# A fused four-layer kernel: attention diagonals as four products, low halves on GpSimd, row dispatch spread over the steps

## The chip, the cores and the metric

The kernel runs on one core of a Trainium2 chip. The metric is the device time of one execution in microseconds. Three runs of the kernel before gave 2604.55, 2605.08 and 2601.78 us. The names of the engines in the profile are PE (TensorE matmuls), PEld (its weight loads), DVE (VectorE), ACT (ScalarE), POOL (GpSimd) and SP (SyncE, which issues most transfers).

## The reference

4096 tokens (16 sequences of 256) of width 128 go through four layers. Every layer normalises its input and adds an attention block and a feed-forward block to it:

```python
xn = _layernorm(x)
x = x + attn_l(xn) + ffn_l(xn)
```

Layer 1 (index 0 in the reference and in the names `L0_...`) has no softmax over keys and a dense feed-forward. The other three have softmax attention with 16 heads in sequences of 256 and a mixture of 8 experts:

- layer 2 (`L1_...`): RMS norm, heads of 64, no mask, two experts of eight for each token;
- layer 3 (`L2_...`): heads of 8, causal mask, one expert for each token;
- layer 4 (`L3_...`): heads of 8 with rotary parts of 32 shared by the heads, causal mask, two experts and a shared one.

```python
probs = softmax(where(mask, (q @ k.T) * scale, -inf)); out = probs @ v
```

## The kernel before

Tokens are worked on in `NCH` = 8 chunks of 512 (two sequences). The stages of the layers with experts are named R, T, A, M and C with the layer index 1, 2 or 3 of the names in the code, so that the *second, third and fourth* layers are A1, A2 and A3: R and T route the tokens, A is the attention, M the experts, C the combination. `stage_closed` makes an engine wait until all engines have left a stage.

**The attention of a chunk** has `STEPS` = 16 steps, one for each pair of heads and sequence (two units a step). A step p goes through the engines like this:

- TensorE `maxima` computes the scores of step p once into the bank pair `duo`; VectorE `maxima` (line 1954) reduces them to the negated row maxima `nmax` (lines 1957 and 1958, in layer 2 line 2077), and makes from them the *diagonals*: the identity times each of four columns of maxima, f16, 128x512 (line 1961, in layer 2 line 2080). It is one `scalar_tensor_tensor` with two inputs in SBUF.
- TensorE `scores` (line 1292) waits for the diagonals, adds them by a matmul to the scores that are computed a second time, with keys on the partitions, in the banks `mo0`, `mo1` and `pt`. So the maximum is subtracted before the exponential.
- ScalarE `exps` (lines 903 and 904) writes each exponential twice, as f32 and as f16: the *high half*.
- The *low half* is the f32 value minus the high half, in f16, so that the products with the values are more exact than f16 alone. In layers 3 and 4 VectorE makes it for both units at once, 128x768 (`pair_low`, line 1967, instruction at 1969). In layer 2 GpSimd makes it, 128x512 for each unit (`prob_low`, line 635, instruction at 637).
- TensorE `average` (line 1318) multiplies both halves with the values into `ob` or `pt`, in small matmuls, once the low half is there. VectorE `scale_o` divides by the row sums.

The order is written out by hand on each engine. In step p of layers 3 and 4 TensorE does scores(p), maxima(p + 2), average(p - 1), then selections, projections or shared-expert work. VectorE does maxima(p + 2) and its diagonals, pair_low(p), then whatever belongs to the chunk (`scale_o`, the residual sum, `prepare` for the next chunk in steps 9 to 13, with the rotary parts of layer 4 at lines 1910 to 1928). ScalarE does exps(p), which waits for the low half of p - 2, since it reuses that buffer. The four halves of two steps share two buffers (`p % 2`).

In layer 2, where VectorE is at maxima(p + 1) in step p, GpSimd waits for the diagonals of step p + 1 before it starts the low halves of step p:

```python
if p + 1 < STEPS or more:
    at_step(diag_made, pool, stage, i, p + 1)
prob_low(i, p, 0)
prob_low(i, p, 1)
```

**Dispatch of rows.** After routing, every token's normalised row must go to the slots of its experts in `slot_rows` in HBM. `send_row_tile` (line 622) sends one tile of 128 rows with an indirect transfer issued by GpSimd. There are 64 tiles in layers 2 and 4 (two experts for each token) and 32 in layer 3. In layer 2 GpSimd sends four after the low halves of each step of the first chunk (`per_step` = 4). In layers 3 and 4 it does nothing else in the attention stage and sends all tiles as soon as the stage opens. SyncE waits for all of a layer's tiles (`rows_sent`) before it loads the next layer's expert weights over the buffer the tiles came from, and the experts stage waits for them too. After layer 3's dispatch GpSimd prepares rotary copies of weights (lines 682 to 684) that TensorE waits for at the start of layer 4's attention, and then sends the experts' results (`send_results`, line 662).

Of the kernel before, what the change touches and what calls it, by code (L numbers as in the profile page):

```python
# [22 lines left out]
ALU = mybir.AluOpType  # L23
# [7 lines left out]
P = 128  # L31
# [4 lines left out]
ALL = TOKENS // P  # L36
# [8 lines left out]
STEPS = 16  # L45
# [97 lines left out]
def build_program(nc, A, out):  # L143
    ctx = ExitStack()
    with ctx:
# [284 lines left out]
        def at_step(event, eng, stage, i, k):  # L430

            per = event.per[stage]
            if k < 0:
                i, k = i - 1, k + per
            elif k >= per:
                i, k = i + 1, k - per
            if not (isinstance(i, int) and i < 0):
                event.wait(eng, stage, i, k)

        def step1(event, eng, i, k):  # L440

            at_step(event, eng, "A1", i, k)
# [150 lines left out]
        def _(pool):  # L593
# [33 lines left out]
            def attention(layer):  # L627

                stage = f"A{layer}"
                stage_closed(pool, f"T{layer}")  # L630
                if layer == 1:
                    pool.wait_ge(blank_sent, 16 * 4 * len(TOP))
                per_step = TOP[layer] * ALL // STEPS

                def prob_low(i, p, h):
                    p_high.wait(pool, "A1", i, 2 * p + h)
                    pool.tensor_tensor(p16[:, p % 2, h, 1, :], p32[:, h, :], p16[:, p % 2, h, 0, :], ALU.subtract)\  # L637
                        .then_inc(p_low.sem, 1)

                def chunk(i, parity, more):  # L640
                    for p in range(STEPS):
                        if p + 1 < STEPS or more:
                            at_step(diag_made, pool, stage, i, p + 1)
                        prob_low(i, p, 0)
                        prob_low(i, p, 1)
                        if isinstance(i, int) and i == 0:
                            for n in range(per_step * p, per_step * p + per_step):
                                send_row_tile(layer, n // ALL, n % ALL)

                if layer == 1:  # L650
                    chunks1(pool, chunk)
                else:
                    for n in range(per_step * STEPS):
                        send_row_tile(layer, n // ALL, n % ALL)

            def send_results(layer):
                def step(s, half, b, first):
# [937 lines left out]
        def _(dve):  # L1595
# [290 lines left out]
            def attention(layer):  # L1886
# [67 lines left out]
                def maxima(i, p):  # L1954

                    max_full.wait(dve, stage, i, 2 * p + 1)
                    dve.tensor_reduce(nmax4[:, p % 2, 0:2], duo[:, :, 0:P], AX.X, ALU.max, negate=True)  # L1957
                    dve.tensor_reduce(nmax4[:, p % 2, 2:4], duo[:, :, P:LINE], AX.X, ALU.max, negate=True)\  # L1958
                        .then_inc(nmax_made.sem, 1)
                    nmax_made.wait(dve, stage, i, p)  # L1960
                    dve.scalar_tensor_tensor(  # L1961
                        out=diag2[:, p % 2, :, :, :].rearrange("p q h c -> p (q h) c"),
                        in0=ident[:, :].rearrange("p (o c) -> p o c", o=1).broadcast_to([P, 4, P]), scalar=1.0 / 16,
                        in1=nmax4[:, p % 2, :].rearrange("p (a o) -> p a o", o=1).broadcast_to([P, 4, P]),
                        op0=ALU.mult, op1=ALU.mult).then_inc(diag_made.sem, 1)

                def pair_low(i, p):
                    p_high.wait(dve, stage, i, 2 * p + 1)
                    dve.tensor_tensor(p16_2[:, p % 2, 1, :], p32_2[:, p % 2, :], p16_2[:, p % 2, 0, :], ALU.subtract)\  # L1969
                        .then_inc(p_low.sem, 1)  # L1970

                def scale_o(i, g):

# [18 lines left out]
                def chunk(i, parity, more):  # L1992
                    begun = not (isinstance(i, int) and i == 0)
                    for p in range(STEPS):
                        if p + 2 < STEPS:
                            maxima(i, p + 2)
                        elif more:
                            maxima(i + 1, p + 2 - STEPS)
                        pair_low(i, p)
                        if p and p % 4 == 0:  # L2000
                            scale_o(i, p // 4 - 1)
                        elif p == 0 and begun:
                            scale_o(i - 1, 3)
                        if p == 2 and begun:
                            add(acc_full, x_made, i - 1, 0)
                        if p == 8 and layer == 3:
                            if begun:
                                x_made.wait(dve, stage, i - 1)
                            add(sh_down, sh_added, i, FB - 1)
                        if more:  # L2010
                            prepare(i + 1, 1 - parity, p)
                    if not more:
                        scale_o(i, 3)
                        if layer == 3:
                            sh_added.wait(dve, stage, i)
                        add(acc_full, x_made, i, 0)
# [202 lines left out]
```

## Time and profile before

| | before |
|---|---|
| median of 3 runs | 2604.55 us |
| lowest and highest | 2601.78 and 2605.08 us |
| the profiled execution's own time | 2598.39 us |
| its span in the profile | 2596.6 us |
| mean granted TensorE clock | 0.883 |
| TensorE matmuls busy | 2019.9 us (78%) |
| TensorE weight loads busy | 1394.1 us (54%) |
| VectorE busy | 1908.6 us (74%) |
| ScalarE busy | 1377.8 us (53%) |
| GpSimd busy | 723.5 us (28%) |

The table is of one execution, taken by the hardware profiler. Weight loads overlap matmuls. Matmul ends are modelled, and spans on GpSimd are rough. The span is the time from the first to the last instruction of the program; the execution's own time is 1.8 us longer. TensorE's clock is given as a share of its full speed. In the rows below, a line of the timeline gives start, duration, engine, source line, operation, output <- inputs, shape and count of merged instructions, and in brackets how long the engine was idle before and who released it. DVEq, SPq and so on are an engine's sequencer.

### The profile page before, as it was taken

What the parts mean: (1) busy time and instruction counts of PE and PEld (TensorE: products, weight loads), DVE (VectorE), ACT (ScalarE), POOL (GpSimd) and SP (SyncE); (2) the same over time, 40 slices, a digit from 0 to 9 for tenths busy, and PEclk for the clock granted to TensorE, in tenths of its full rate; (3) what the DMA queues carried; (4) which work ended last, traced back from release to release, by engine and by line L of the source; (5) the groups of instructions that cost most, each with busy time, mean ns of one, the idle gap of its engine ahead of it and who ended that gap; (6) DMA issues with size and microseconds to landing.
All of it is one profiled execution on the core that took longest, in us unless ns stands there. A gap on an engine that the chain in (4) does not pass through costs nothing.

```text
span 2596.6 us, 65873 instructions
## 1 busy us (share of the span) xinstructions
PE 2019.9 (78%) x23246; PEld 1394.1 (54%) x23247; DVE 1908.6 (74%) x4031; ACT 1377.8 (53%) x2794; POOL 723.5 (28%) x674
## 2 busy tenths in 40 slices
PE   1543679999999788815888887863899999998993
PEld 0213346666666566714555554543566666665662
DVE  2236667878788788866999998766677777776775
ACT  0231346767677655502766666430566666665552
POOL 0012685545455333323300000340720000000552
PEclk9775889999999999965988987885899998998997
DMA  8900012000000011220200000120100000000224
GB/s 226 168 0 0 26 37 72 2 3 3 3 2 2 10 48 49 61 73 15 85 2 2 2 2 5 48 64 12 51 18 2 2 2 2 2 2 10 63 62 124
DMA packets 109664, 88.07 MB, mean 34 GB/s; under 512 B 11240, under 2 KB 95816, under 8 KB 109424
## 3 DMA queue, kind: packets, MB, share of 16 engines
q1 hardware_dynamic: 97840, 60.82, 9.8%
q0 software_dynamic: 11584, 23.91, 2.7%
q8 instruction: 168, 2.75, 0.4%
q14 instruction: 72, 0.59, 0.1%
HBM read 45.26 MB, written 39.43 MB: 33 GB/s over the span
## 4 chain that ended last, share of the span: by engine, by line
PE 48%; DVE 28%; issue 12%; POOL 6%; ACT 3%; DMA 2%; DVEq 1%; SPq 1%; ACTq 0%; POOLq 0%
PE duo L1020 11%; PE mo L1020 10%; PE misc L1020 9%; PE acc L1020 6%; PE ob L1020 6%; DVE v L1969 4%; PE pt L1020 4%; DVE nmax L1958 3%; POOL slot_rows L623 2%; DVE nmax L2077 2%; DVE v L1802 2%; DVE nmax L1957 1%; DVE v L1794 1%; DVE region L2080 1%; DVE qT L1961 1%
## 5 line engine op out<-in xcount | busy, mean ns | idle before, releaser
L662 POOL DMA_INDIRECT results<-probT,dest_no x202 | 210.7, 1043 | 1158.5 <-ACT probT L701 1121.9
L637 POOL TENSOR_TENSOR v<-v 128x512 f16<-128x512 f32 x256 | 290.7, 1157 | 299.0 <-DVE region L2080 298.3
L1020 PE MATMUL ob<-wm,v 128*128 128x9 f16 (+1 forms) x5856 | 254.9, 180 | 72.8 <-DVE v L1969 48.9
L1020 PEld LDWEIGHTS ob<-wm,v 128*128 128x128 f16 x5856 | 222.6, 97 | 130.7 <-DVE v L1969 74.0
L903 ACT ACTIVATE v<-mo 128x384 f32<-128x384 f32 x352 | 174.2, 495 | 166.8 <-PE mo L1020 91.8
L961 ACT ACTIVATE v<-mo 128x512 f32<-128x512 f32 x256 | 153.4, 599 | 204.1 <-PE mo L1020 138.0
L1969 DVE TENSOR_TENSOR v<-v 128x768 f16<-128x768 f32 x256 | 243.5, 951 | 11.8 <-ACT v L904 11.8
L2077 DVE TENSOR_REDUCE nmax<-duo 128x2 f32<-128x512 f32 x256 | 164.8, 685 | 87.9 <-PE duo L1020 87.8
L1020 PE MATMUL duo<-kT,wm 128*128 128x256 f16 x1212 | 172.7, 279 | 55.0 <-DVE kT L1790 29.2
L1957 DVE TENSOR_REDUCE nmax<-duo 128x2 f32<-128x256 f32 x256 | 107.7, 421 | 133.6 <-PE duo L1020 132.8
L1020 PE MATMUL mo<-qT,kT 64*128 64x256 f16 (+1 forms) x2240 | 202.3, 274 | 0.0
L623 POOL DMA_INDIRECT slot_rows<-xd,slot_no x160 | 164.7, 1030 | 129.9 <-DVEq L1773 83.9
L1961 DVE SCALAR_TENSOR_TENSOR qT<-ident,nmax 128x512 f16<-128x512 f32 x256 | 177.2, 692 | 8.8
L904 ACT ACTIVATE v<-mo 128x384 f16<-128x384 f32 x352 | 175.7, 499 | 0.0
L1958 DVE TENSOR_REDUCE nmax<-duo 128x2 f32<-128x512 f32 x256 | 173.9, 679 | 0.0
L815 ACT ACTIVATE v<-duo,cols 128x256 f32<-128x256 f32 x248 | 103.9, 470 | 105.8 <-PE duo L1020 88.2
L1020 PEld LDWEIGHTS duo<-kT,wm 128*128 x1212 | 113.1, 99 | 81.9 <-issue 66.7
L962 ACT ACTIVATE v<-mo 128x512 f16<-128x512 f32 x256 | 153.1, 598 | 0.0
L1020 PE MATMUL pt<-region,v 128*128 128x65 f16 x3072 | 118.7, 194 | 35.8 <-POOL v L637 35.8
L1020 PEld LDWEIGHTS mo<-qT,kT 64*128 64x128 f16 (+1 forms) x2240 | 94.9, 96 | 95.4 <-issue 87.8
L1020 PE MATMUL duo<-kT,qT 64*128 64x256 f16 (+2 forms) x1536 | 141.6, 264 | 1.8 <-DVE nmax L1958 1.1
L1794 DVE TENSOR_TENSOR v<-v 128x512 f16<-128x512 f32 x202 | 139.1, 689 | 4.4 <-ACT v L701 0.2
(277 smaller groups left out, 4642.8 us busy)
## 6 DMA issues: line engine op xcount, KB each, us to landing
prob<-slot_rows SPq DMA_DIRECT2D x101, 130.0 KB
qT<-results SPq DMA_DIRECT2D x40, 256.0 KB, 3.1
slot_rows<-prob SPq DMA_DIRECT2D x4, 1300.0 KB, 18.6
slot_rows<-prob SPq DMA_DIRECT2D x4, 1235.0 KB, 20.1
xd<-in_L_ffn_w_dram SPq DMA_DIRECT2D x2, 2048.0 KB, 12.4
results<-probT,dest_no POOLq DMA_INDIRECT x202
slot_rows<-xd,slot_no POOLq DMA_INDIRECT x160, 2.3
x<-in_L_attn_x_dram SPq DMA_DIRECT2D x8, 256.0 KB, 4.6
```

The costliest lines, as they stand in the source:

```text
L623: pool.indirect_dma_start(out=slot_rows[layer], out_offset=bass.IndirectOffsetOnAxis(ap=slot_no[:, j, t:t + 1], axis=0), in_=xd[:, t, :], ...
L637: pool.tensor_tensor(p16[:, p % 2, h, 1, :], p32[:, h, :], p16[:, p % 2, h, 0, :], ALU.subtract)\
L662: pool.indirect_dma_start(out=results[layer], out_offset=bass.IndirectOffsetOnAxis(ap=dest_no[:, 2 * b + t:2 * b + t + 1], axis=0), in_=y_ ...
L903: act.activation(p32_2[:, p % 2, own], src, ACT.Exp)
L904: act.activation(p16_2[:, p % 2, 0, own], src, ACT.Exp).then_inc(p_high.sem, 1)
L961: act.activation(p32[:, h, :], mo[h][:, :], ACT.Exp)
L1020: return pe.matmul(dst, lhsT, rhs, start=start, stop=stop)
L1794: dve.tensor_tensor(hb[:, h, 1, :], hid[:, h, :], hb[:, h, 0, :], ALU.subtract)\
L1958: dve.tensor_reduce(nmax4[:, p % 2, 2:4], duo[:, :, P:LINE], AX.X, ALU.max, negate=True)\
L1961: dve.scalar_tensor_tensor(out=diag2[:, p % 2, :, :, :].rearrange("p q h c -> p (q h) c"), in0=ident[:, :].rearrange("p (o c) -> p o c", o ...
L1969: dve.tensor_tensor(p16_2[:, p % 2, 1, :], p32_2[:, p % 2, :], p16_2[:, p % 2, 0, :], ALU.subtract)\
L2077: dve.tensor_reduce(nmax[:, 2 * (p % 2) + h, :], sco[h][:, :].rearrange("p (q k) -> p q k", q=2), AX.X, ALU.max, negate=True).then_inc(nma ...
```

## The change

In layers 3 and 4 the diagonals become four `tensor_scalar` instructions of 128 columns, each with one column of maxima as its per-partition scalar. The low halves of these layers move from VectorE to GpSimd, still as one instruction of 128x768 for a step, after the step's exponentials and with no wait for the diagonals. GpSimd's attention loop is one for all three layers, written out over all 8 x 16 steps, and sends one tile after the low halves of each step until all are sent: 64 steps in layers 2 and 4, 32 in layer 3. In layer 2 the low halves keep their wait for the diagonals. What GpSimd does after the attention (the rotary copies) comes after the last low half of layer 3.

```diff
@@ gpsimd, attention(layer)
-                per_step = TOP[layer] * ALL // STEPS
+                n_tiles = TOP[layer] * ALL
 
                 def prob_low(i, p, h):
                     p_high.wait(pool, "A1", i, 2 * p + h)
                     pool.tensor_tensor(p16[:, p % 2, h, 1, :], p32[:, h, :], p16[:, p % 2, h, 0, :], ALU.subtract)\
                         .then_inc(p_low.sem, 1)
 
-                def chunk(i, parity, more):
+                def pair_low(i, p):
+                    p_high.wait(pool, stage, i, 2 * p + 1)
+                    pool.tensor_tensor(p16_2[:, p % 2, 1, :], p32_2[:, p % 2, :], p16_2[:, p % 2, 0, :], ALU.subtract)\
+                        .then_inc(p_low.sem, 1)
+
+                for i in range(NCH):
                     for p in range(STEPS):
-                        if p + 1 < STEPS or more:
-                            at_step(diag_made, pool, stage, i, p + 1)
-                        prob_low(i, p, 0)
-                        prob_low(i, p, 1)
-                        if isinstance(i, int) and i == 0:
-                            for n in range(per_step * p, per_step * p + per_step):
-                                send_row_tile(layer, n // ALL, n % ALL)
-
-                if layer == 1:
-                    chunks1(pool, chunk)
-                else:
-                    for n in range(per_step * STEPS):
-                        send_row_tile(layer, n // ALL, n % ALL)
+                        if layer == 1:
+                            if p + 1 < STEPS or i < NCH - 1:
+                                step1(diag_made, pool, i, p + 1)
+                            prob_low(i, p, 0)
+                            prob_low(i, p, 1)
+                        else:
+                            pair_low(i, p)
+                        n = i * STEPS + p
+                        if n < n_tiles:
+                            send_row_tile(layer, n // ALL, n % ALL)
@@ vector, attention(layer)
                     nmax_made.wait(dve, stage, i, p)
-                    dve.scalar_tensor_tensor(
-                        out=diag2[:, p % 2, :, :, :].rearrange("p q h c -> p (q h) c"),
-                        in0=ident[:, :].rearrange("p (o c) -> p o c", o=1).broadcast_to([P, 4, P]), scalar=1.0 / 16,
-                        in1=nmax4[:, p % 2, :].rearrange("p (a o) -> p a o", o=1).broadcast_to([P, 4, P]),
-                        op0=ALU.mult, op1=ALU.mult).then_inc(diag_made.sem, 1)
-
-                def pair_low(i, p):
-                    p_high.wait(dve, stage, i, 2 * p + 1)
-                    dve.tensor_tensor(p16_2[:, p % 2, 1, :], p32_2[:, p % 2, :], p16_2[:, p % 2, 0, :], ALU.subtract)\
-                        .then_inc(p_low.sem, 1)
+                    for n in range(4):
+                        ins = dve.tensor_scalar(diag2[:, p % 2, n // 2, n % 2, :], ident[:, :], nmax4[:, p % 2, n:n + 1],
+                                                1.0 / 16, ALU.mult, ALU.mult)
+                    ins.then_inc(diag_made.sem, 1)
@@ vector, attention(layer), chunk
                             maxima(i + 1, p + 2 - STEPS)
-                        pair_low(i, p)
                         if p and p % 4 == 0:
```

## Rows read from the trace of the kernel before

**Rows 1.** The page's busy time, share of the span and instructions of each engine.
```profile
PE 2019.9 (78%) x23246; PEld 1394.1 (54%) x23247; DVE 1908.6 (74%) x4031; ACT 1377.8 (53%) x2794; POOL 723.5 (28%) x674
```

**Rows 2.** Windows, core 0: stretch, length, busy of PE PEld DVE ACT POOL, clock, DMA.
```profile
277.28:396.49 119.21, 84.43 (x943) 55.06 (x941) 78.56 (x113) 51.40 (x97) 101.52 (x96) 0.87 0.11 36
396.49:881.00 484.51, 458.01 (x6340) 324.22 (x6340) 395.67 (x749) 342.40 (x665) 251.52 (x222) 0.99 0.04 11
1227.37:1610.43 383.06, 330.44 (x4604) 212.93 (x4600) 352.48 (x627) 261.42 (x600) 28.35 (x46) 0.90 0.05 17
1841.67:2378.42 536.75, 517.37 (x6070) 347.67 (x6069) 412.49 (x711) 365.38 (x703) 48.45 (x46) 0.94 0.02 7
```

**Rows 3.** Timeline of POOL in the first chunk of layer 2's attention.
```profile
307.25 2.27 POOL L637 TENSOR_TENSOR v<-v 128x512 f16<-128x512 f32 x2
309.68 1.25 POOL L623 DMA_INDIRECT slot_rows<-xd,slot_no  x1 [0.17 <-ACT v L962]
...
315.01 2.28 POOL L637 TENSOR_TENSOR v<-v 128x512 f16<-128x512 f32 x2
```

**Rows 4.** Waits from 271 to 400 us: total, times, longest.
```profile
ACT v L961 <- POOL v L637: 65.8, 16, 4.6
```

**Rows 5.** Source line 637 from 397 us (first and last start), and a later POOL timeline.
```profile
L637 POOL TENSOR_TENSOR v<-v x224: 1147/1157/1165, 396.5 to 883.0; 128x512 f16<-128x512 f32 x112
...
421.17 2.27 POOL L637 TENSOR_TENSOR v<-v 128x512 f16<-128x512 f32 x2 [1.41 <-DVE region L2080]
```

**Rows 6.** Timeline of DVE in a plain step of layer 3.
```profile
1402.86 0.42 DVE L1957 TENSOR_REDUCE nmax<-duo 128x2 f32<-128x256 f32 x1
...
1403.91 0.69 DVE L1961 SCALAR_TENSOR_TENSOR qT<-ident,nmax 128x512 f16<-128x512 f32 x1
1404.52 0.95 DVE L1969 TENSOR_TENSOR v<-v 128x768 f16<-128x768 f32 x1
1405.39 0.42 DVE L1957 TENSOR_REDUCE nmax<-duo 128x2 f32<-128x256 f32 x1
```

**Rows 7.** Waits from 1227.37 to 1610.43 us (layer 3's attention).
```profile
PE ob L1020 <- DVE v L1969: 44.0, 76, 0.9
```

**Rows 8.** Timelines of PE and of ACT in that plain step.
```profile
1403.00 0.60 PE L1020 MATMUL ob<-wm,v 128*128 128x9 f16 x18 [0.84 <-DVE v L1969]
1403.46 0.33 PE L1020 MATMUL mo<-qT,sixteen 128*128 128x256 f16 x2
...
1404.54 0.39 PE L1020 MATMUL duo<-mask,ident 128*128 128x256 bf16 x2
...
1404.47 0.49 ACT L903 ACTIVATE v<-mo 128x384 f32<-128x384 f32 x1 [1.15 <-PE pt L1020]
...
1405.60 0.51 ACT L904 ACTIVATE v<-pt 128x384 f16<-128x384 f32 x1
```

**Rows 9.** Normalisation, line 1646, alone and beside POOL's pair: timelines and source view.
```profile
341.81 1.10 DVE L1646 TENSOR_SCALAR tmp<-x,mv,rstd 128x128 f32<-128x128 f32 x4
...
434.79 1.96 DVE L1646 TENSOR_SCALAR tmp<-x,mv,rstd 128x128 f32 x4
...
L1646 DVE TENSOR_SCALAR tmp<-x,mv,rstd x4: 334/336/1193, 434.8 to 436.4; 128x128 f32 x4
...
433.88 2.27 POOL L637 TENSOR_TENSOR v<-v 128x512 f16<-128x512 f32 x2 [2.24 <-DVE region L2080]
```

**Rows 10.** Waits from 1841.67 to 2378.42 us (layer 4's attention).
```profile
DVE nmax L1957 <- PE duo L1020: 106.2, 88, 3.3
...
PE misc L1020 <- DVE wm L1928: 17.3, 7, 2.5
```

**Rows 11.** Timeline of DVE where layer 4's projections are made.
```profile
2103.10 0.69 DVE L1918 TENSOR_TENSOR prob<-prob 128x512 f32<-128x512 f32 x1
```

**Rows 12.** Timeline of POOL after layer 3's attention; its copies, by line and form.
```profile
1642.55 1.32 POOL L662 DMA_INDIRECT results<-probT,dest_no  x1 [380.43 <-ACT probT L701]
...
L682 POOL COPY region<-region 128x32 f32<-128x32 f32 x8 | 3.1, 390 | 0.0
```

## The prediction

> **What bounds the kernel now.** I read the page first, then the windows of the three attention stages, then, stage by stage, the waits and the timeline of single steps. On the page TensorE is busy 78% of the span, VectorE 74% and GpSimd 28% [rows 1]: an average that hides three different stages [rows 2]. The first chunk of layer 2's attention takes 119.21 us, with GpSimd busy for 101.52 us and TensorE's clock at 0.87. The other seven chunks take 484.51 us, clock 0.99. Layer 3's attention takes 383.06 us, TensorE busy 86% and VectorE 92%. Layer 4's takes 536.75 us, TensorE busy 96%.
>
> *Layer 2, first chunk: GpSimd is the bound.* Its timeline shows a pair of low halves (2.27 us) and four transfers between 307.25 and 315.01, back to back [rows 3]. Meanwhile ScalarE waits 65.8 us in 16 steps for the low halves [rows 4]. From 396.49 the same pairs come every 4.37 us ((881.9 - 396.5) / 111 steps; the last record starts at 883.0 and is the second of its pair), and GpSimd has 1.41 us idle even before the pairs that come soonest [rows 5].
>
> *Layer 3: VectorE is the bound.* A plain step is four instructions without a gap: two maxima, the diagonal (start to start 0.61 us) and the low half (0.87 us); the next step begins after 2.53 us [rows 6]. TensorE waits 44.0 us in 76 places for the low half [rows 7]. The mean step is 383.06 / 127 = 3.02 us [rows 2].
>
> *Layer 4: TensorE is the bound.* VectorE waits 106.2 us for TensorE's maxima; the other way there is only one wait worth its name, 17.3 us for the values' low half (line 1928), at the end of the projections, where VectorE is late [rows 10].
>
> **The change, part by part.**
>
> *1. Layer 2's transfers, four a step for 16 steps, become one a step for 64 steps.* The first chunk falls from 119.2 us to that of the later ones, 16 x 4.37 = 69.9: minus 49. The price in the other 48 steps: a transfer takes 0.17 + 0.96 to 1.25 us behind a pair [rows 3], and GpSimd is idle for 1.41 us in the shortest steps [rows 5]: it fits, barely, and what is late by 0.1 us meets no one, because TensorE and ScalarE hardly wait for the low halves there. The first chunk has fewer tail operations of a chunk before it, the last sends may meet VectorE: between minus 50 and minus 40, I take **minus 47**. SyncE loads the next experts' weights once all rows are sent, now some 150 us later but still over 300 us before the stage ends. Cost none; if this cover went, the loads would be exposed.
>
> *2. Layers 3 and 4: the low half leaves VectorE.* Per step 0.87 us less there, 128 steps in each layer. On GpSimd 128x512 takes 1.16 us and two in a row 2.27 us [rows 3]; 768 columns are 1.5 times that, 1.67 to 1.74: I take 1.7. The shape itself isn't in the trace; between 1.16 and 2.3 (two instructions' worth).
>
> *3. The diagonal as four products of 128 columns.* The nearest row is the normalisation (a product with per-partition scalars, 128x128): four take 1.10 us, so 0.25 us from start to start and 0.34 us for the last [rows 9]. Two scalars there, one here; f32 out there, f16 here. Bounds: 0.61 us for all four (what the single instruction takes now) and 1.10. I take 1.0: VectorE pays 0.4 us more. Together with 2 VectorE is freed of 0.46 us a step.
> The Trainium skill (VectorE: DVE Perf Modes, the section on the TRN2 errata) says that each instruction with its source in SBUF pays a fixed extra cost, so that operands should have 512 elements or more: a rule against this split. Its own formula, 58 cycles plus half a cycle for each element in the doubled mode, would give four products an estimated 0.51 us, less than the row's 1.10; by it the collision below would be 0.5 us shorter and layer 3 would end some 20 us earlier than I say. The measured row decides for me.
>
> *4. The collision, since nothing waits for the diagonals.* Rows 9 show it: at 434.79 four such products ran beside GpSimd's pair (433.88 to 436.15), and together they took 1.96 us, not 1.10; one of them took 1.193 us, to the end of the pair. So a product that meets GpSimd's low half stands still until that is done. In layer 2 the wait for the diagonal keeps the two apart; the new code for layers 3 and 4 has no such wait.
>
> *5. Layer 3's step, put together.* Follow a low half to the one two steps later (same row buffers, same order on TensorE). From its end: 0.06 us to the averaging matmuls, 0.46 to the next scores, 1.01 to the exponentials, 1.64 for the four of them (1404.47 to 1405.60 + 0.51) [rows 8], 0.17 to GpSimd [rows 3], 1.7 for the low half: 5.04 us for two steps, **2.52 a step**, against 2.53 now. The gain on VectorE is thus eaten by GpSimd's length. Now the collision: the maxima end about when the exponentials do, so the products stand until the low half ends, then need 0.05 + 3 x 0.25 + 0.34 = 1.15 us; the scores wait for them and begin 1.2 us after the low half instead of 0.52. That gives 5.72 for two steps, **2.86 a step**. GpSimd then is free for 1.1 us a step, just what the products need, so this repeats.
> Steps with other work: TensorE is busy 330.44 / 127 = 2.60 us a step, against 1.93 in a plain one (1403.00 to the end of the masks at 1404.93 [rows 8]), so some 10.7 us a chunk is extra. It lies between averaging and scores, where 0.7 us of it is hidden by the wait for the diagonals; I put half of it as hidden, and of the rest one chain of every second step meets about half: 3 us. A chunk becomes 16 x 2.86 + 3 = 48.8 us against 48.3 now (16 x 3.02). Eight chunks: plus 4 us. Its 32 transfers make GpSimd's step 1.7 + 0.17 + 1.0 + 0.17 = 3.04 us, a little over 2.86: plus 4 at most. Together **plus 8 us**; bounds minus 25 (2.52 a step and TensorE's own work, 45.5 us a chunk) and plus 40 (3.3 a step).
>
> *6. Layer 4.* The mean step is 4.22 us, TensorE works 4.07 of it [rows 2]; the chain of 5, with a half microsecond more for its longer scores, is near 3.2. TensorE's work is the cover. If it were gone, each step would cost up to 0.3. What shows is the stretch of projections, where VectorE is nearly full: it gains 0.46 us a step in four steps, and loses up to 1.7 us where the sum of the rotated parts and their low halves (two inputs in SBUF, line 1918 [rows 11]) or the products meet GpSimd; two such steps a chunk. The wait of 17.3 us can go, or double. I take **plus 6 us**, between minus 15 and plus 20.
>
> *7. GpSimd's copies for the rotary weights* (24 in three kinds, the longest 0.39 us in the mean) now come after layer 3's attention. The first result of the experts leaves at 1642.55, 30 us after that attention, so they are hidden [rows 12]; nobody else needs them before layer 4. Zero.
>
> **Sum.** -47 + 8 + 6 = -33 us. The profiled execution took 2598.4 us (span 2596.6, 1.8 around it), 6.2 below the median of 2604.55. The change would profile at 2565; in the median of runs, **2572**.
>
> **Rivals.**
> *Freed VectorE wins (0.22).* The products don't collide, because one scalar and an f16 output behave otherwise or because the maxima end before the exponentials. For it: VectorE is the bound of layer 3 and its relief is real. Against it: 0.34 us beside 1.193 in one and the same four [rows 9]. Layer 3 goes to 45.5 us a chunk (minus 22), layer 4 loses its wait (minus 17): 2604.5 - 47 - 39 = 2518; half of it, about 2540.
> *Port queue (0.10), slower.* GpSimd's low half itself waits for the products, which then stand in the chain of layer 3 once more: 5.72 + 1.0 = 6.7 for two steps, 3.36 a step, 54 a chunk with little hidden: plus 70 with the extras, and 10 in layer 4: 2604.5 - 47 + 80 = 2637. The point from which it decides is a mean step in layer 3 of 3.02 + 41 / 127 = 3.34 us (layer 4 as forecast). Against it: beside GpSimd's pairs VectorE waited, never the pair (2.27 us throughout).
> *Spreading saves little (0.03), slower.* If one transfer a step moved every pair by 1 us, 48 steps would give the 47 back: 2604.5 + 14 = 2618. Against it: 1.41 us idle.
> *Weak gain (0.10):* layers 3 and 4 cost 25 to 40 together, 2583 to 2597. *Nothing to see (0.05).*
>
> **How the numbers follow.** The forecast has 0.50. A measurement of this kernel tells 0.2% (5 us) from no change. Faster is 0.50 + 0.22 + 0.10 = 0.82, same 0.05, slower 0.13. The range goes from 2528, inside the first rival, to 2612, which covers plus 40 in layer 3 with plus 15 in layer 4: about 2 in 10 lie outside.
>
> **What would show it.** Right: the first chunk of layer 2 near 70 us, the pairs with one transfer between them and no wait of ScalarE for GpSimd; in layers 3 and 4 some of the 1,024 products at over 1 us and most at 0.3; the diagonals as the wait in front of layer 3's scores, in place of VectorE's low half in front of the averaging; 2.8 to 2.9 us in plain steps; layer 4 within 10 us of 537. Wrong: products all short (then the first rival), GpSimd's low halves of uneven length (the second), or pairs in chunks two to four of layer 2 later than 4.4 us apart.

## The result and the profile after: 0.8% slower

The kernel before gave a median of 2603.16 us in four runs, the changed one 2623.11 us in four (2620.68 to 2625.71). The ratio is 1.0079, 95% interval [1.0063, 1.0095]. A repetition in another set of runs gave 1.0107 [1.0069, 1.0145]. Slower was on record with a chance of 0.13, and 2623 is above the range.

Stages are measured here from the first exponentials of the first step to those of the last, in the profiled execution (before, after):

| | before | after | change | forecast |
|---|---|---|---|---|
| layer 2's attention | 606.2 | 555.5 | -50.7 | -47 |
| layer 3's attention | 382.3 | 434.7 | +52.4 | +8 |
| layer 4's attention | 536.0 | 550.9 | +14.9 | +6 |
| all else | 1072.1 | 1077.7 | +5.6 | 0 |

Busy time of the changed kernel, from its page (beside [rows 1]):

```profile
PE 2050.4 (78%) x23246; PEld 1405.4 (54%) x23247; DVE 1945.7 (74%) x4543; ACT 1373.7 (52%) x2794; POOL 1145.2 (44%) x930
```

VectorE lost 256 low halves, each 0.87 us from start to start, and is yet busy for 37 us more than before. That alone says that the products do something else than compute.

The same windows as [rows 2], of the changed kernel: stretch, length, busy of PE, PEld, DVE, ACT and POOL, clock, DMA.

```profile
276.40:345.20 68.80, 65.13 (x884) 44.61 (x880) 56.84 (x107) 49.15 (x96) 50.79 (x47) 0.98 0.05 16
345.20:831.90 486.70, 462.52 (x6404) 327.62 (x6401) 398.28 (x757) 342.11 (x671) 300.27 (x272) 0.99 0.06 18
1180.40:1615.10 434.70, 372.06 (x4586) 230.70 (x4582) 400.55 (x879) 260.94 (x598) 239.26 (x159) 0.78 0.05 16
1846.80:2397.80 551.00, 518.41 (x6054) 346.12 (x6052) 423.78 (x963) 364.78 (x702) 276.22 (x191) 0.95 0.03 10
```

Layer 2's first chunk is as short as the others. In layer 3 TensorE is busy for 372 us instead of 330 with the same matmuls, and its granted clock fell from 0.90 to 0.78.

GpSimd's timeline in layer 2's first chunk (beside [rows 3]):

```profile
311.99 2.26 POOL L637 TENSOR_TENSOR v<-v 128x512 f16<-128x512 f32 x2 [0.29 <-DVE region L2075]
314.42 0.99 POOL L623 DMA_INDIRECT slot_rows<-xd,slot_no  x1 [0.16 <-issue]
316.50 2.33 POOL L637 TENSOR_TENSOR v<-v 128x512 f16<-128x512 f32 x2 [1.10 <-DVE region L2075]
```

One transfer a step leaves GpSimd idle before every pair. ScalarE's wait of [rows 4] is gone from the long waits of that stretch.

Layer 3: the source views of the products and of GpSimd's low halves (minimum, median, longest in ns), then the waits of 1180.4 to 1615.1 us (total, times, longest; beside [rows 7]) and one of layer 4 (beside [rows 10]).

```profile
L1964 DVE TENSOR_SCALAR qT<-ident,nmax x506: 271/275/1753, 1180.3 to 1612.7; 128x128 f16<-128x128 f32 x169
...
L642 POOL TENSOR_TENSOR v<-v x127: 1627/1641/1747, 1182.2 to 1614.7; 128x768 f16<-128x768 f32 x127
```
```profile
PE ob L1022 <- POOL v L642: 26.8, 35, 1.2
...
PE ob L1022 <- DVE tmp L1976: 20.1, 28, 1.7
...
PE mo L1022 <- DVE qT L1964: 13.5, 13, 1.4
...
PE misc L1022 <- DVE wm L1930: 22.3, 7, 3.2
```

The diagonals of layer 3 by line, busy time and the mean of one in ns, in the kernel before and in the changed one:

```profile
L1961 DVE SCALAR_TENSOR_TENSOR qT<-ident,nmax 128x512 f16<-128x512 f32 x127 | 88.0, 693 | 4.4
...
L1964 DVE TENSOR_SCALAR qT<-ident,nmax 128x128 f16<-128x128 f32 x506 | 246.2, 546 | 5.8 <-issue 1.3
```

They take 158 us more of VectorE's time, and the low halves that left it took 121. VectorE is as full as before: 400.55 of 434.70 us, against 352.48 of 383.06 [rows 2].

Products last up to 1.75 us while GpSimd's low half keeps its 1.64 us: VectorE waits for GpSimd, not the other way. The timelines of VectorE, GpSimd and TensorE in a few steps of layer 3:

```profile
1416.26 0.87 DVE L1964 TENSOR_SCALAR qT<-ident,nmax 128x128 f16<-128x128 f32 x4
1418.09 1.64 POOL L642 TENSOR_TENSOR v<-v 128x768 f16<-128x768 f32 x1 [3.08 <-ACT v L906]
1418.25 0.48 PE L1022 MATMUL mo<-qT,sixteen 128*128 128x256 f16 x2
1418.65 1.75 DVE L1964 TENSOR_SCALAR qT<-ident,nmax 128x128 f16<-128x128 f32 x4
...
1424.22 0.33 PE L1022 MATMUL mo<-qT,sixteen 128*128 128x256 f16 x2
1425.02 3.66 DVE L1964 TENSOR_SCALAR qT<-ident,nmax 128x128 f16<-128x128 f32 x4
1425.19 3.41 POOL L642 TENSOR_TENSOR v<-v 128x768 f16<-128x768 f32 x2 [1.89 <-ACT v L906]
1428.74 0.34 PE L1022 MATMUL mo<-qT,sixteen 128*128 128x256 f16 x2 [0.80 <-DVE qT L1964]
```

Alone, four products take 0.87 us. At 1418.65 the first of them stands until the low half ends (1.75 for the four). At 1425.02 two low halves came one after the other, and two of the four products stood, each behind one: 3.66 us. Of the 128 groups of layer 3, 85 hold one product over 0.8 us, 13 hold two, 30 none, and the mean group lasts 1.94 us. In layer 4, 76 of 128 hold one. Each of these 187 long products ends 0.08 or 0.09 us after the end of a low half. The two matmuls into `mo` take 0.48 us at 1418.25, where the granted clock is 0.50, and 0.33 at 1424.22, where it is 1.00: TensorE at its lower and at its upper clock, inside ten microseconds.

### The profile page after: what moved, and what is told of

Read it like the earlier page. It is cut to its first block, busy times and chain, and to the rows that moved or that the text cites. A ratio compares the mean times of both kernels' runs of the same rounds, so it can differ in the third digit from the quotient of the medians.

```text
span 2618.8 us, 66430 instructions
## 1 busy us (share of the span) xinstructions
PE 2050.4 (78%) x23246; PEld 1405.4 (54%) x23247; DVE 1945.7 (74%) x4543; ACT 1373.7 (52%) x2794; POOL 1145.2 (44%) x930
## 4 chain that ended last, share of the span: by engine, by line
PE 49%; DVE 28%; issue 12%; POOL 3%; ACT 3%; DMA 2%; DVEq 1%; SPq 1%; ACTq 0%; POOLq 0%
PE duo L1022 11%; PE mo L1022 10%; PE misc L1022 9%; PE acc L1022 6%; PE ob L1022 6%; DVE qT L1964 5%; PE pt L1022 4%; DVE nmax L1960 3%; DVE nmax L2072 2%; DVE v L1804 2%; DVE region L2075 1%; DVE v L1796 1%; POOL v L642 1%; DVE x L1874 1%; DVE nmax L1959 1%
## 5 line engine op out<-in xcount | busy, mean ns | idle before, releaser
L642 POOL TENSOR_TENSOR v<-v 128x768 f16<-128x768 f32 x256 | 424.4, 1658 | 577.3 <-ACT v L906 574.8
L1964 DVE TENSOR_SCALAR qT<-ident,nmax 128x128 f16<-128x128 f32 x1024 | 443.7, 493 | 10.4 <-issue 1.3
L1022 PE MATMUL mo<-qT,sixteen 128*128 128x256 f16 x704 | 128.5, 271 | 13.9 <-DVE qT L1964 13.5
```

The lines of the kernel that those rows point to most:

```text
L642: pool.tensor_tensor(p16_2[:, p % 2, 1, :], p32_2[:, p % 2, :], p16_2[:, p % 2, 0, :], ALU.subtract)\
L1022: return pe.matmul(dst, lhsT, rhs, start=start, stop=stop)
L1964: ins = dve.tensor_scalar(diag2[:, p % 2, n // 2, n % 2, :], ident[:, :], nmax4[:, p % 2, n:n + 1], 1.0 / 16, ALU.mult, ALU.mult)
```

## The experiments

Sixteen kernels in four sets, each set with the kernel before beside it. In two sets the kernel before took 2602 to 2603 us, in the two others 2715 (last section). So stages of the profiles are compared below, and a ratio only inside its set. A stage's time is that of one trace. Repeated traces differ by up to 5 us (c_before, c_after below), and layer 4 in two kernels with the same code there by up to 7. Layers 3 and 4 stand with the granted clock in brackets:

| label | diagonal | low half | layer 3, us | layer 4, us | ratio |
|---|---|---|---|---|---|
| before | one | VectorE | 382.3 (0.90) | 536.0 (0.94) | |
| after | four | GpSimd | 434.7 (0.78) | 550.9 (0.95) | 1.0079 |
| e1_dispatch | one | VectorE | 416.0 (0.82) | 577.6 (0.91) | 0.9805 |
| e2_products | four | VectorE | 445.8 (0.77) | 563.2 (0.92) | 1.0138 |
| e3_single | one | GpSimd | 427.3 (0.74) | 546.6 (0.95) | 0.9615 |
| e4_wait | four | GpSimd, waits | 462.5 (0.69) | 537.1 (0.99) | 1.0115 |
| e5_psum | one, PSUM | GpSimd | 394.7 (0.82) | 508.3 (1.00) | 0.9417 |
| e9_psum_split | four, PSUM | GpSimd | 442.1 (0.72) | 549.7 (0.94) | 1.0065 |
| with the fill in layer 3: | | | | | |
| e8_before_fill | one | VectorE | 365.1 (0.99) | 531.2 (0.95) | 0.9919 |
| e12_products_fill | four | VectorE | 406.6 (0.95) | 557.3 (0.93) | 1.0012 |
| e11_single_fill | one | GpSimd | 384.6 (0.99) | 553.1 (0.94) | 0.9502 |
| e7_after_fill | four | GpSimd | 410.3 (0.95) | 553.4 (0.94) | 0.9987 |
| e14_wait_fill | four | GpSimd, waits | 419.8 (0.95) | 535.6 (1.00) | 0.9628 |
| e13_psum_split_fill | four, PSUM | GpSimd | 399.1 (0.98) | 547.4 (0.95) | 0.9595 |
| e6_psum_fill | one, PSUM | GpSimd | 362.6 (1.00) | 507.4 (1.00) | 0.9624 |
| e10_burst | one, PSUM | GpSimd, after a burst | 379.9 (0.96) | 564.0 (0.95) | 0.9913 |

The ratios of e3, e5, e11, e13 and e14 are against 2715 and flatter them by about 4%; those of e1, e2 and e12 are not, since these kernels keep the burst. These three contain the stall of their sets instead: the first step of layer 3 takes 29, 27 and 27 us in them, that of layer 4 48, 18 and 18, against 3 to 5 us elsewhere.

**The parts alone.** The kernel before with one part of the change each.

```diff
@@ e1: gpsimd, attention(layer), with the changed loop over i and p below it, for layer 2
+                if layer > 1:
+                    for n in range(n_tiles):
+                        send_row_tile(layer, n // ALL, n % ALL)
+                    return
@@ e2: vector, maxima
-                    dve.scalar_tensor_tensor(
...
+                    for n in range(4):
+                        ins = dve.tensor_scalar(diag2[:, p % 2, n // 2, n % 2, :], ident[:, :], nmax4[:, p % 2, n:n + 1],
+                                                1.0 / 16, ALU.mult, ALU.mult)
```

> Only the dispatch of layer 2 is spread to one transfer a step; layers 3 and 4 are as before. If the parts add up, layer 2's attention ends some 50 us earlier, as in the changed kernel (606 to 555 us), and nothing else moves: ratio near 0.980 (2552 us). If instead the spread transfers are what hurts later stages (later weight loads, an unrolled GpSimd program), part of the 50 us comes back and the ratio is above 0.985.

> The kernel before with only the diagonals of layers 3 and 4 as four products; low halves stay on VectorE, so GpSimd's low halves cannot meet them. Port theory (the loss comes from meeting GpSimd): no product above 0.3 us outside the 32 and 64 transfers, four of them take 0.87 us against 0.69, so 0.2 us a step where VectorE is the bound: layer 3's attention from 382 to about 405 us, layer 4's by 0 to 5, ratio 1.010. Split theory (the four short instructions themselves are the loss): most of the 52 us is already here, layer 3 near 430.

e1 took 2661.23 us against 2714.98: 0.9805 [0.9786, 0.9824]. Layer 2's attention took 555.5 us, to the tenth what the whole change has there. Step 1 is settled. e2 gave 1.0138 [1.0091, 1.0184]: the split costs with no low half on GpSimd beside it, all products at 0.28 us. Its first chunk in layer 3 takes 74.0 us and the six after it 54.0 in the mean. Without these 20 us of stall layer 3 would be near 426 us: what the split theory gave, and 20 above the port theory.

**One part taken out of the changed kernel.**

```diff
@@ e3: vector, maxima
-                    for n in range(4):
-                        ins = dve.tensor_scalar(diag2[:, p % 2, n // 2, n % 2, :], ident[:, :], nmax4[:, p % 2, n:n + 1],
...
+                    dve.scalar_tensor_tensor(
...
@@ e4: gpsimd, layers 3 and 4
+                            if p + 2 < STEPS or i < NCH - 1:
+                                at_step(diag_made, pool, stage, i, p + 2)
                             pair_low(i, p)
@@ e5: as e3, and
+                dve.tensor_copy(duo[:, 0, LINE:CHUNK], ident[:, :]).then_inc(v_ones2, 1)
...
-                        in0=ident[:, :].rearrange("p (o c) -> p o c", o=1).broadcast_to([P, 4, P]), scalar=1.0 / 16,
+                        in0=duo[:, 0, LINE:CHUNK].rearrange("p (o c) -> p o c", o=1).broadcast_to([P, 4, P]), scalar=1.0 / 16,
@@ e5: tensor, maxima
-                    at_step(nmax_made, pe, stage, i, p - 1)
+                    at_step(diag_made, pe, stage, i, p - 1)
```

> The changed kernel with the diagonals as the one instruction of before (two inputs in SBUF), low halves on GpSimd without a wait. Port theory: that instruction meets GpSimd's low half as well, but only once, so it never waits for two of them; layer 3 is between the two kernels, 400 to 425 us, and single instructions of 1.5 to 2.4 us are seen. Split theory: the loss goes with the split, layer 3 at or below 385 us. Length theory (GpSimd's 1.64 us in place of 0.95 in the chain is the loss, the meeting costs nothing): layer 3 as in the changed kernel, 430 to 440 us.

> The changed kernel, but in layers 3 and 4 GpSimd waits for the diagonals of step p + 2 before the low half of step p, as layer 2 does for its own. Port theory: no product over 0.4 us any more, but the wait puts the low half behind maxima and products: layer 3 between 400 and 435 us, layer 4 at 530 to 545. Length theory: it only adds a wait, layer 3 at 450 us or more.

> The changed kernel, but the diagonals are one instruction that reads the identity from 128 free columns of a PSUM bank, so that it has one input in SBUF; TensorE's maxima wait for the diagonals before them, in place of the maxima before them. Port theory: it never waits for GpSimd (0.68 us each), the two-step chain of 5.0 us holds, layer 3 takes about 365 us (16 x 2.52 plus extra work, a chunk of 45.5), layer 4 530, the ratio is near 0.97 (2525 us), and TensorE's granted clock in layer 3 is back at 0.88 or more. Length theory: layer 3 stays at 425 us or more.

e3: the single instruction, with two inputs in SBUF, stands as well (73 of 126 over 0.8 us, up to 2.53), and layer 3 is 7 us shorter than with the products, little more than traces of one kernel differ. e4: hardly a product stands (7 over 0.8 us), and layer 3 is 28 us *longer*, since now the low half stands in line: above the 400 to 435 of the port theory, and as the length theory had it. Layer 4, where TensorE is the bound, is 14 us shorter with this wait (537.1). So in layer 3 the two bodies of work on VectorE and GpSimd cost time whichever waits. e5: with the identity in PSUM the diagonal takes 0.69 us each time. Layer 3 falls to 394.7 us, not to the 365 of the port theory, and layer 4 to 508.3, below its 530 and 28 below the kernel before. The windows of e5, layers 3 and 4:

```profile
1184.00:1578.70 394.70, 355.83 (x4586) 221.20 (x4586) 251.67 (x500) 258.90 (x599) 239.54 (x159) 0.82 0.06 18
1818.40:2326.70 508.30, 494.57 (x6054) 337.45 (x6052) 301.21 (x584) 364.73 (x702) 272.32 (x191) 1.00 0.03 10
```

TensorE is busy for 494.6 us in layer 4, against 517.37 before [rows 2], with the same matmuls. At a clock of 0.94 those 517 were no measure of its work.

**The clock.** In each of these kernels layer 3 has a clock of at most 0.90, and the longer it takes, the lower mostly the clock. The next runs give TensorE more to do: three matmuls a step into a region of `ob` that nobody reads, ahead of its wait for the low half in layer 3 (the *fill*).

```diff
+if layer == 2:
+    for _n in range(3):
+        mm(ob[:, SEQ:CHUNK].rearrange("p (a c) -> p a c", a=2), sixteen16[:, :],
+           twice(sixteen16[:, :]), True, True)
 p_low.wait(pe, stage, i, p)
```

> The kernel before once more, for its trace on the chip of this job: the chip of the first job ran it 4% slower than the one it was first timed on, and the kernels there that still send all rows of layers 3 and 4 at once stood still for 8 to 50 us at the start of those attentions. If that depends on the chip, this trace shows such stalls where the kernel takes near 2715 us, and none where it takes near 2605.

> The changed kernel on the chip of this job. Its stages are as in its first trace everywhere: 555, 435 and 551 us for the three attentions, near 2620 us in all. So against the kernel before: ratio 1.008 on a chip where that takes 2605 us, and 0.965 where it takes 2715 us, since one transfer a step leaves no burst.

> The kernel with the identity in PSUM, and in layer 3 three more matmuls of 256 columns on constants before every averaging, whose result nobody reads (0.33 us a step at the full clock), where TensorE waits for the low half anyway. Clock theory: a good part of layer 3's time is TensorE at its lower clock; with the gaps filled the granted clock there goes from 0.82 to 0.92 or more and the attention of layer 3 gets shorter than 395 us, by 10 to 30 us, with 40 us of work more. Chain theory (the clock only follows): it stays at 395 us or gets longer by up to 30.

> The changed kernel with three matmuls of 256 columns more before each wait of TensorE for the low half in layer 3; their result is read by nobody. It asks how much of the +52 us in layer 3 is TensorE's clock (0.78 there, 0.90 before) and how much the chain with its collisions. Clock theory: the clock of layer 3 rises to 0.9 or more and its attention falls from 435 to 400 or 415 us, although TensorE has more to do; the whole run gets 20 to 35 us shorter than the changed kernel and ends below the kernel before. Chain theory: the products still wait for GpSimd (about 110 of them over 0.8 us), the step is set by ScalarE, GpSimd and VectorE, whose clock is fixed, and layer 3 stays at 430 or more, or grows by the fill. Both agree that the long products stay.

> The kernel before with the same three matmuls in layer 3. It asks whether the kernel before, too, lost time to the clock (0.90, or 0.87 in its second profile). If VectorE is its bound, as I read it (2.53 us in a plain step, four instructions without a gap), a full clock changes little: layer 3 at 370 to 385 us, the run within 10 us of the kernel before. If the clock was the bound there as well, layer 3 falls below 365, as in the run with the identity in PSUM and the fill (362.6).

c_before (2606.06 us; layer 3 387.1, clock 0.87) and c_after (2629.40; 435.9, clock 0.78) repeat the first pair. e6, which is e5 with the fill, took 2503.33 us against 2603.3: 0.9624 [0.9587, 0.9661]. Its layer 3 has more work than that of e5 and is 32 us shorter. The layer 3 windows of e7 and of e8:

```profile
1183.40:1593.70 410.30, 354.92 (x4966) 246.69 (x4962) 380.44 (x879) 260.90 (x599) 240.14 (x159) 0.95 0.06 17
```
```profile
1230.80:1595.90 365.10, 338.64 (x4966) 237.47 (x4962) 351.37 (x627) 261.07 (x599) 25.80 (x44) 0.99 0.06 17
```

The fill takes 24 us off layer 3 in the changed kernel (434.7 to 410.3) and 17 off in the kernel before (382.3 to 365.1). My expectation for e8 was that VectorE's bound would leave it above 370: a miss, as the whole run shows too, 0.9919 [0.9894, 0.9945]. Both theories were partly right: of the 52 us, 7 are the change in what the clock costs (4 by the second pair of traces, 48.8 in place of 52.4), and 45 remain at a clock of 0.95 and more. The fill adds matmuls, so it need not give back all that the clock had cost. e7 is level with the kernel before (0.9987 [0.9969, 1.0005]). Its waits in layer 3, and e8's beside them:

```profile
PE ob L1022 <- DVE tmp L1980: 39.2, 31, 2.6
```
```profile
PE ob L1020 <- DVE tmp L1984: 14.7, 24, 1.1
```

Before the averaging of each fourth step TensorE waits for `scale_o` to have emptied `ob`, and `scale_o` is queued on VectorE behind products that stand.

**Without the standing, split kept.**

```diff
@@ e9: as e5, and
+                    for n in range(4):
+                        ins = dve.tensor_scalar(diag2[:, p % 2, n // 2, n % 2, :], duo[:, 0, LINE:CHUNK], nmax4[:, p % 2, n:n + 1],
+                                                1.0 / 16, ALU.mult, ALU.mult)
```

> The four products are kept, but the identity is read from a copy in PSUM, so that no product has to wait for GpSimd. It separates the split itself from the collision. Collision theory: all 1,024 products are near 0.3 us, none above 0.8; four of them last 0.9 to 1.1 us against 0.69 for the single instruction from PSUM, so layer 3 comes out some 5 to 20 us above the 394.7 of that run and at least 15 us below the 436 of the changed kernel; layer 4 near 510. If the source in PSUM were not what frees them, long products remain and layer 3 stays near 436.

All products take 0.34 us, four of them 1.13, and none stands. Yet layer 3 is 442.1 us, not 400 to 415: a miss. TensorE waits 52.0 us in 71 places for the products before its next maxima, the wait that came with the PSUM copy, and its clock is 0.72, the lowest but one. Two things moved at once, so this run decides nothing. The rest was done with the fill.

**What the 45 us are made of.** Four runs, all with the fill: e12 is e2 with it, e11 is e3, e13 is e9, e14 is e4.

> The kernel before with only the split (four products, low halves left on VectorE) and the fill. No product can meet GpSimd. VectorE is the bound at full clock (365.1 us, 2.875 a step with the single instruction); four products take 0.26 us more from start to start, so a step becomes 3.13 and layer 3 about 398 us if the split pays in full, 365 to 375 if VectorE had room.

> The changed kernel with the single instruction for the diagonal in place of the four products, and the fill: the move of the low halves alone. Theory that the waiting for GpSimd makes the 45 us: the single instruction waits too (some 70 of 126 over 0.8 us) and layer 3 is 395 to 410 us. Theory that the split makes them: layer 3 falls to 365 to 375.

> Four products with the identity in PSUM, low halves on GpSimd, fill: split and move without waiting for GpSimd. Its chain is maxima on TensorE, two reductions, four products (1.13 us), then the next maxima: 2.94 us in a step read at full clock. So 375 to 385 us in layer 3 if collisions are what the changed kernel suffers from, all products at 0.34 us. If the split is the cost by itself, it stays near 410.

> The changed kernel with GpSimd's wait for the diagonals of step p + 2 before the low half of step p (the way layer 2 has it), and the fill. No product waits, but the low half does: products and low half stand in one line. At a clock of 0.69 that gave 3.64 us a step; at full clock I expect 3.1 to 3.3 us, 395 to 420 in layer 3, so no better than the collisions.

e12's first chunk has the stall of its set (71.7 us); the six after it take 48.4 us each, against 46.0 in e8. Without the stall (71.7 - 48.4 = 23.3) its layer 3 is 383.3 us: the split alone costs 18, where I had expected up to 33. From the first of its products to the start of the low half behind them it is 0.79 us, against 0.61 with the single instruction. e11: the move alone costs 384.6 - 365.1 = 19.5. That is between what the two theories gave, and the reason was expected by neither. Its source view of the low half, and a step, in which VectorE was first:

```profile
L642 POOL TENSOR_TENSOR v<-v x127: 1634/2024/2162, 1181.8 to 1562.4; 128x768 f16<-128x768 f32 x127
```
```profile
1471.80 0.69 DVE L1967 SCALAR_TENSOR_TENSOR qT<-ident,nmax 128x512 f16<-128x512 f32 x1
1471.97 2.02 POOL L642 TENSOR_TENSOR v<-v 128x768 f16<-128x768 f32 x1 [0.69 <-ACT v L906]
```

Here GpSimd stands: the low half started 0.17 us behind the diagonal and took 2.02 us instead of 1.64. Only 10 of 126 diagonals stood. Of the 110 low halves over 1.75 us in layers 3 and 4, 109 end 1.50 us after the end of the instruction of VectorE that was running when they started. In e3, 62 low halves of layer 3 stand in the same way. Who comes second waits. The Trainium skill (SBUF — State Buffer, section "SBUF: two separate sides") gives this as a rule: whichever of the two starts first holds the shared pair of ports for its whole instruction, and a VectorE operation counts when it runs in a two-port mode or has two inputs in SBUF. The runs here agree: 1.51 us in the median for a product of the changed kernel's layer 3 that came second, 2.02 for a low half of e11.

e13 (399.1 us) misses the expected 375 to 385, and is 11 below e7 although it has a wait of its own and slower products. So standing costs at least that. With the single instruction the same exchange (e11 to e6) takes 22 us off layer 3 and 46 off layer 4. e14 is 10 above e7, as expected: the wait is the dearer way in layer 3 with the fill too, while layer 4 is again shorter with it (535.6 against 553.4). And e6 (362.6) against e8 (365.1) says what the move is worth in layer 3 when nothing stands and the diagonal stays one instruction: 2.5 us at full clock, no more than two traces of one kernel differ, for TensorE is then busy for 343 of 363.

Split and move alone cost 18 and 19.5 us, both together 45. Taken step by step, 31 of these 45 us lie between the exponentials of steps 1 and 2, 5 and 6, 9 and 10, 13 and 14 of the chunks. There TensorE averages step 0, 4, 8 or 12, with its wait for `scale_o`. The twelve other steps of a chunk share 14. That wait is 2.8 us in e11 and 19.1 in e12, so it needs both parts to become 39.2. This fits the queue behind standing products; no run takes `scale_o` out of that queue, so its share isn't measured by itself.

Without the fill the parts add up even less: layer 3 is near 426 us in e2 and 427.3 in e3, so either part alone costs 44 or 45 of the 52. The fill is worth about 40 us in e2, e3, e4 and e9, where the clock was 0.69 to 0.77.

**The price of the burst.** e6 with the transfers of layers 3 and 4 in one row ahead of GpSimd's first low half.

```diff
+if layer > 1:
+    for n in range(n_tiles):
+        send_row_tile(layer, n // ALL, n % ALL)
...
-                        if n < n_tiles:
+                        if layer == 1 and n < n_tiles:
```

> The fastest version so far (identity in PSUM, fill), with the transfers of layers 3 and 4 in one burst at the start of the attention, as in the kernel before, now ahead of GpSimd's first low half. GpSimd then starts its first low half 32 transfers of about 1.2 us later in layer 3 and 64 later in layer 4, so TensorE and ScalarE stand for that time: about +35 us in layer 3 and +75 in layer 4 if the low halves must wait for the burst, about 2610 us in all. It prices spreading in layers 3 and 4, which the change needs as soon as the low halves are on GpSimd. The rival: the transfers can be issued faster than one in 1.2 us when none waits, and the price is under half of that.

```profile
1185.16 0.96 POOL L623 DMA_INDIRECT slot_rows<-xd,slot_no  x1 [0.30 <-issue]
1186.42 0.96 POOL L623 DMA_INDIRECT slot_rows<-xd,slot_no  x1 [0.30 <-issue]
```

It took 2580.82 us; layer 3 379.9 (+17) and layer 4 564.0 (+57). The transfers do come every 1.26 us, but layer 3's burst begins at 1167.33, 17 us before the stage's first exponentials (1184.1), which I had not counted. In layers 3 and 4 the spreading is what pays for low halves on GpSimd: it saves 74 us that a burst ahead of the low halves would bring.

## Why the prediction was wrong, step by step

- **Step 1 (layer 2, -47)** was right: -50.7, and -50.6 in e1's form of it alone. The last sends met VectorE without a price.
- **Step 2 (1.7 us for the low half)** was right: 1.64.
- **Step 3 (four products, 1.0 us)** measured 0.87, or 0.79 from start to start against 0.61 for the single instruction (e12): VectorE pays 0.18 us a step, not 0.4. The Trainium skill's formula (VectorE: DVE Perf Modes, the section on the TRN2 errata) gives an estimate of 0.51 us, well below 0.87. Its advice to give an instruction 512 elements or more held, at 0.69 for one against 0.87 for four.
- **Step 4 (the collision)** was right in kind: a product stands until GpSimd is done. That it can happen twice in one group (13 times) was not foreseen.
- **Step 5 (layer 3, +8, bounds -25 and +40)** is the step that failed, by 44 us (41 by the second pair). Its path was wrong. It let the scores wait for the diagonals in every step and counted 2.86 us for a plain one. TensorE's matmuls wait there for only 13.5 us in 13 places, where 0.7 us in each of 127 steps would be 89. Before the averaging they wait 26.8 us for the low half and 20.1 for `scale_o`. The missing term is what is queued behind a standing product. I followed scores and low halves. By my own figures 2.86 us leave VectorE nothing but maxima (1.05), products (1.15) and standing (the rest), and its other work, `scale_o`, the residual sum and `prepare`, 37 us in this stage, has no place in the sum. As an estimate, 37 / 127 = 0.29 us more make a step 3.15, and e7 has 3.23. With the fill on both sides (e7 against e8) the change costs 45 us: 37 of the miss are here. The other 7 are TensorE's clock, which no term of the sum held. I read 0.90 in [rows 2] and took VectorE for the bound all the same; e8 shows that 17 us of those 382 were the clock's already. The runs that put more waits into the chain have the lowest clocks (e4 0.69, e9 0.72), and each matmul in the chain then takes longer: the 0.48 us in place of 0.33.
- **Step 6 (layer 4, +6)** measured +14.9, inside its bounds (+19.5 by the second pair). Its cover was read wrong: "TensorE works 4.07 of 4.22" was partly the clock (0.94). In e5 the same work takes 494.6 us and the layer 508.3. The wait at the end of the projections grew from 17.3 us to 22.3.
- **Step 7 (rotary copies, 0)**: nothing in the stretch between the layers moved (232.0 us before, 231.7 after).

The rivals: *port queue* gave 2637 and a mean step over 3.34 us; the step came out at 3.42. But what it named, GpSimd waiting for the products, is not in the changed kernel's layer 3 (1.64 us, at most 1.75), so its time is near for another reason. It is in e3 and e11, where the diagonal is one longer instruction. *Freed VectorE wins* would have needed e5's PSUM copy and the fill: its 45.5 us a chunk are 364 in layer 3, and e6 has 362.6.

## What to carry over

When work goes from VectorE to GpSimd, ask of every VectorE instruction beside it where its inputs lie: what stood here stopped standing with one input in PSUM. A wait between the two was dearer than the collision in layer 3, where VectorE is the bound, and cheaper in layer 4, where TensorE is. Follow not only the chain through the standing instruction but all that is queued behind it. And read the granted clock of a stage before its busy shares: at 0.90 TensorE's busy time is inflated, so it is no measure of what that engine covers. A few matmuls nobody reads, put ahead of a wait, gave 17 to 43 us back.

## What the runs showed that was not expected

- Both kernels were partly bound by TensorE's clock. The fastest version, e6 (spread transfers, identity in PSUM, single diagonal, low halves on GpSimd, fill), beats the kernel before by 3.8% [3.4%, 4.1%]. TensorE's granted clock is 1.00 in both layers, which is its 2.4 GHz level; the two levels are seen in the change itself as 0.33 and 0.48 us for the same pair of matmuls. The Trainium skill (TensorE: Matmul & The Clock Gate, Part 1) calls the slow level the state of an idle array, which activity lifts. The fill runs agree: with three matmuls more a step, layer 3 goes from 0.82 (e5) to 1.00 (e6).
- In two sets the kernel before took 2715 us. There, kernels that send layer 3's and 4's rows in a burst stall at the start of those layers, on a releaser outside the program's semaphores; e12's layer 3 shows it:

```profile
DVE nmax L1961 <- remote: 27.4, 2, 15.3
```

  Kernels with one transfer a step (e3, e5, e11, e13, e14) have no such stall there. That the burst holds up the loading of instructions is only a guess. In e1 no packet of the instruction queue is seen between 1812 and 1901 us, while GpSimd issued its 64 transfers, and in e2 and e12 there are such pauses of 93 and 87 us over layer 4's burst; in the kernel before at 2605 us packets came during it, with at most 28 us between them. What makes a set behave like this stays open. It matters for the judgement: where the kernel before takes 2715, the changed one is likely the faster (e3, which differs from it in the diagonal alone, gave 0.9615 there), but it was not run there itself; in the sets where it was run, it is slower by 0.8 and 1.1%.
